# Two edge sums: fp32 rows stored in source order and gathered in destination order, in place of three bf16 parts scattered

## The chip, the cores and the metric

The kernel runs on one core of a Trainium2 chip. The metric is the time of one execution on the device, in microseconds.

## The reference, cut to what matters

A graph of 6250 nodes with 48 features and 200000 edges goes through four message-passing blocks, each followed by a layer norm. The change touches the last two, which are sums over edges of rows of x:

```python
def _L2_gnn_ref(x, edge_index, edge_weights):
    row, col = (edge_index[0], edge_index[1])
    ...
    norm = edge_weights / jnp.sqrt(deg[row] * deg[col])
    msg = x[row] * norm[:, None]
    out = jax.ops.segment_sum(msg, col, num_segments=N)

def _L3_gnn_ref(label_mat, edge_index, num_nodes):
    ...
    norm = deg_inv_sqrt[row] * deg_inv_sqrt[col]
    msgs = label_mat[row] * norm[:, None]
    out = jax.ops.segment_sum(msgs, col, num_segments=num_nodes)
```

The square roots of the degrees are multiplied into node rows before and after, so each block is: take the row y[src] of every edge (in the first of the two, times the edge's weight) and add it to the sum of dst.

## The kernel before, in words

The first phases (not touched, except for one) sort the edges into granules of GR = 4 edges that share a block of 128 nodes, once by source block and once by destination block. There are NS = 456 columns of 128 granules in either order. The phase edge_keys (called keys in the profile) computes these orders while GpSimd (POOL) gathers table rows, 34 columns a chunk, and ScalarE (ACT) stores them as raw. Its SyncE (SP) queue also fills tensors in DRAM with zeros, among them the whole of messages, k.msg: 171 stores of 384 KB at L334. k.place[p, u] is the place in destination order of a granule of the source order, k.origin the row in source order of a granule of the destination order.

The sums are the two stages at the end of program: next_tables (node rows y and their split in three bf16 parts, k.y3), then a spread, a tally, and combine. The weighted sum uses spread (stage 1), the plain sum spread_plain (stage 2); both are called spread in the profile.

Spread works in 76 chunks of EX = 6 columns, four chunks to a turn of the loop. For each chunk SP loads the one-hot matrices of the source lanes (oht, 384 KB); ACT reads a block number from irow and copies that block's three parts to table, six times; TensorE (PE) expands them to edges; VectorE (DVE) evicts; POOL scatters six times 128 granules to k.msg at place. In spread PE adds the three parts up in PSUM (72 matmuls of 48 columns a chunk, L2460), DVE multiplies by the weights (six at L2475) and splits the product again in three bf16 parts (split, L880 to L883) that go to out. In spread_plain PE passes the parts through (24 matmuls of 144 columns, L2566) and DVE copies them to out in 12 halves (L2582). POOL's scatters (L692) run after the copy of the chunk's part of place (L2478, L2578). out has a ring of four buffers, and DVE waits for the scatters of the chunk four before.

Tally also works in 76 chunks of six columns, two chunks to a turn. SP loads 864 KB of k.msg, in destination order and contiguous (L2615), DVE builds the one-hot matrices of the destination lanes (hot, 3072 elements a lane, L2650), PE sums with 72 matmuls of 48 columns (L2629), ACT evicts 288 elements to k.parts (L2639). POOL does nothing.

A phase of a different purpose, expand (L1506 to L1592, four times in the program), has nearly the structure that spread has after the change: 76 chunks of six columns, oht of 384 KB loaded by SP, 72 matmuls a chunk (of 52 columns), six evictions to fp32, and a 624 KB store by SP. Its table copies are shared between ACT and POOL, three each.

## Time and profile before

| | us |
|---|---|
| median of 3 runs | 19494.06 (19445.77 to 19525.49) |
| profiled execution, its own time | 19660.36 |
| span of the profiled execution | 19658.6 |
| spread 1 (weighted), first work to last landing | 17305 to 18053 |
| tally 1, up to its last eviction | 18053 to 18356 |
| spread 0 (plain) | 18450 to 19257 |
| tally 2 | 19257 to 19566 |

The span is the time between the first and the last instruction of one execution on the core; 1.8 us of its own time lie outside it. The stages run one after another with a barrier between, so what a stage gains or loses moves the end by as much. Busy time is summed by engine over a stretch; a group of instructions is one line, one operation and one shape.

### The profile page before, as it was taken

Reading aid. Unit: us, or ns where it says so; the run is one execution under the profiler, and the core shown is the slowest. Engines: PE = TensorE matmul, PEld = TensorE weight load, DVE = VectorE, ACT = ScalarE, POOL = GpSimd, SP = SyncE. Lnnn points to the kernel's source line nnn. Section 1 sums busy time; section 2 is a strip of 40 time slices with the busy share of each in tenths; the row PEclk is TensorE's granted clock in tenths of the full one; section 3 lists DMA queues with packets and bytes.
Section 4 is the critical chain, followed back from the end, with each engine's and each line's share of the span. In section 5 each row is a group of like instructions: output and inputs, shape, how many; then the busy total and the mean of one; then the engine's idle time right before and its main releaser. Section 6 shows DMA issues by size and latency. Waiting matters only on the chain. (4 is left out here: it accounts for less than half of the span.)

```text
span 19658.6 us, 403615 instructions
## 1 busy us (share of the span) xinstructions
PE 10605.2 (54%) x119643; PEld 8071.2 (41%) x119643; DVE 11207.2 (57%) x26701; ACT 5226.6 (27%) x15775; POOL 9060.3 (46%) x10645
## 2 busy tenths in 40 slices
PE   1001046666666337965884786598255555534334
PEld 1001024444444017864774776587233333323213
DVE  6557034445445456875886787588433333356647
ACT  0000012222222004642662454266122222211110
POOL 7778654444444623432441342244354545465251
PEclk9855555555555559987996997799666666655656
DMA  4552344444445227545552754655111111134434
GB/s 133 171 188 68 90 77 72 73 73 73 73 74 71 45 49 224 160 111 178 158 159 73 213 158 103 183 158 159 45 41 44 41 44 41 40 104 141 131 116 150
DMA packets 2548256, 2116.07 MB, mean 108 GB/s; under 512 B 418326, under 2 KB 2314030, under 8 KB 2541161
## 3 DMA queue, kind: packets, MB, share of 16 engines
q1 hardware_dynamic: 2164318, 1438.64, 25.0%
q0 software_dynamic: 309216, 539.49, 15.1%
q10 hardware_dynamic: 74552, 135.95, 2.1%
q8 instruction: 73, 1.20, 0.0%
q14 instruction: 97, 0.79, 0.0%
HBM read 1290.57 MB, written 726.03 MB: 103 GB/s over the span
## 5 line engine op out<-in xcount | busy, mean ns | idle before, releaser
L686 POOL DMA_INDIRECT attend_rows<-key_rows,attend_fetch_now x1824 | 1752.7, 961 | 2434.4 <-PE attend_seg L1717 2108.7
L686 POOL DMA_INDIRECT edges_rows<-raw,edges_perm_now x1824 | 1765.6, 968 | 2032.1 <-issue 1650.0
L1761 ACT ACTIVATE attend_hot<-attend_lane_hot,attend_share 128x128 f32<-128x128 fp8e4 x7296 | 2227.0, 387 | 110.6 <-DVE attend_share L1784 79.2
L686 POOL DMA_INDIRECT mlp_xin<-table,mlp_staged x1564 | 1492.1, 954 | 1483.7 <-PEq L2308 1023.5
L686 POOL DMA_INDIRECT keys_rows<-table,keys_staged x1564 | 1873.5, 1198 | 541.0 <-issue 541.0
L1717 PE MATMUL attend_seg<-attend_rows,attend_hot 128*128 128x49 f32 x14592 | 1884.3, 284 | 73.5 <-issue 39.1
L1717 PEld LDWEIGHTS attend_seg<-attend_rows,attend_hot 128*128 128x128 f32 x14592 | 1809.1, 201 | 115.2 <-issue 109.7
L1704 PE MATMUL attend_qx<-attend_table,attend_oht 128*128 128x90 bf16 x21888 | 1132.8, 211 | 441.7 <-DMA attend_oht<-src_hots 374.8
L692 POOL DMA_INDIRECT messages<-spread_out,spread_place_now x912 | 1024.8, 1124 | 603.0 <-issue 475.9
L1704 PEld LDWEIGHTS attend_qx<-attend_table,attend_oht 128*128 128x128 fp8e4 x21888 | 1036.7, 103 | 507.8 <-issue 506.4
L1801 DVE TENSOR_REDUCE attend_mraw<-attend_top 128x2 f32<-128x1024 f32 x912 | 1111.1, 1218 | 84.9 <-issue 48.4
L1093 PE MATMUL edges_ps_t<-ident,edges_attr 128*40 128x128 f32 x1824 | 430.4, 414 | 1232.8 <-issue 681.6
L2310 PE MATMUL mlp_ps<-mlp_xT,mlp_w 112*128 112x512 f32 (+1 forms) x828 | 598.9, 814 | 864.6 <-issue 776.5
L1211 DVE TENSOR_TENSOR edges_dot<-edges_ps_e,edges_rows 128x256 f32<-128x256 f32 x228 | 96.8, 425 | 1596.0 <-remote 1564.8
L1528 POOL COPY expand_table<-k 128x156 bf16 x912 | 291.3, 319 | 1527.1 <-PEq L1565 799.8
L1093 PEld LDWEIGHTS edges_ps_t<-ident,edges_attr 128*40 128x40 f32 x1824 | 244.3, 144 | 1681.3 <-issue 1607.1
L864 DVE TENSOR_TENSOR_SCAN mlp_sums<-keepr,mlp_sums,mlp_val 128x34 f32<-128x34 f32 x2208 | 502.4, 278 | 711.6 <-issue 707.9
L1577 PE MATMUL expand_ps<-expand_table,expand_oht 128*128 128x52 bf16 x21888 | 645.4, 188 | 474.4 <-DVE expand_out L1590 311.5
L1125 PE MATMUL edges_ps<-edges_eT,edges_w 40*48 40x512 f32 x912 | 831.2, 1056 | 47.7 <-issue 47.1
L1792 DVE TENSOR_REDUCE attend_score<-attend_prod 128x8 f32<-128x720 f32 x912 | 823.6, 903 | 31.5
L1590 DVE COPY expand_out<-expand_ps 128x208 f32<-128x208 f32 x1824 | 543.8, 366 | 502.4 <-DMA key_rows<-expand_out 300.1
L1110 PE MATMUL edges_ps<-edges_w,edges_act 49*128 49x48 f32 x3648 | 829.7, 412 | 0.0
(542 smaller groups left out, 23412.1 us busy)
## 6 DMA issues: line engine op xcount, KB each, us to landing
key_rows<-expand_out SPq DMA_DIRECT2D x304, 624.0 KB
attend_ea<-edge_attrs SPq DMA_DIRECT2D x912, 160.0 KB
tally_rows<-messages SPq DMA_DIRECT2D x152, 864.0 KB, 4.9
attend_table<-q SPq DMA_DIRECT2D x1832, 67.5 KB
expand_oht<-dst_hots SPq DMA_DIRECT2D x304, 384.0 KB
attend_oht<-src_hots SPq DMA_DIRECT2D x912, 128.0 KB
attend_lane_hot<-src_hots_by_edge SPq DMA_DIRECT2D x912, 128.0 KB
raw<-keys_rows ACTq DMA_DIRECT2D x46, 2176.0 KB
```

The source lines that it names most:

```text
L686: return nc.gpsimd.indirect_dma_start(out=out, out_offset=None, in_=table, in_offset=bass.IndirectOffsetOnAxis(ap=index, axis=0))
L692: return nc.gpsimd.indirect_dma_start(out=table, out_offset=bass.IndirectOffsetOnAxis(ap=index, axis=0), in_=rows, in_offset=None, bounds_ ...
L1093: ins = nc.tensor.transpose(ps_t[0:RBF, u, c * P:(c + 1) * P], attr[p][:, u, c * RBF:(c + 1) * RBF], k.ident[:])
L1110: ins = mm(ps_2[:, (u * GR + c) * F:(u * GR + c + 1) * F], act1[0:F + 1, u, c * P:(c + 1) * P], w2[:], start=True, stop=True)
L1125: ins = mm(ps_1[0:F, u, :], w1[:], eT[:, u, :], start=True, stop=True)
L1577: ins = nc.tensor.matmul(ps[u][:, c * KROW:(c + 1) * KROW], oht8[b][:, u, c::GR], table[b][:, u, j, :], start=(j == 0), stop=(j == 2))
L1704: ins = mm(qx[b % 2][:, u, c * QROW:(c + 1) * QROW], oht8[b][:, u, c::GR], table[b % 3][:, u, j, :], start=(j == 0), stop=(j == 2))
L1717: ins = mm(seg2[:, u, 0:SUMS], hot[p % 2][:, u, c, :], rows4[p][:, u, c, 0:SUMS], start=(c == 0), stop=(c == GR - 1))
L1761: ins = nc.scalar.activation(hot[p][:, u, c, :], lane_hot8[r][:, u, c, :], ACT.Copy, scale=share[p][:, u, c:c + 1])
L1792: ch.done(v.tensor_reduce(score[b % 3][:].rearrange("p u c -> p (u c)"), prod[:].rearrange("p u c w -> p (u c) w"), AX, ALU.add))
L1801: v.tensor_reduce(mraw[:], top[:], AX, ALU.max).then_inc(s_read, 1)
L2310: nc.tensor.matmul(ps_1[1 - q][:, 0:w], w1[:], xT[1 - q][0:X, 0:w], start=True, stop=True).then_inc(s_1, 1)
```

## The change

Both sums use one spread with fp32 output and one tally. Spread now evicts the 192 elements a lane and column to fp32 (times the weight in stage 1, a plain copy in stage 2), six instructions a chunk, and SP stores the chunk, 576 KB, in source order to k.rows_a, where each partition has its own contiguous stretch. POOL has no work there, and DVE no split. SP loads two chunks ahead and stores behind each load.

Tally's POOL gathers 128 granules of 768 bytes at a time from k.rows_a at k.origin, six times a chunk, into a ring of four fp32 buffers. ACT rounds the chunk (1152 elements a lane) to bf16, DVE subtracts that in place, ACT rounds the rest, DVE subtracts again into the third part. DVE's one-hot matrices are as before, between its two subtractions, and PE has the same 72 matmuls. DVE also copies the part of origin for the chunk three ahead, and ACT's eviction of the chunk before stands between its two roundings. Both loops have four chunks to a turn, with the first and last four outside the loop.

In edge_keys the 171 zero stores to k.msg are gone, and one store clears the row that each partition of k.rows_a has past its 456.

```diff
-MSG = 3 * F
-ZW = 1536
-ZEROS = NS * GR * MSG // ZW
-assert ZEROS * ZW == NS * GR * MSG and ZW // 2 <= C // 2 * F
...
-            with sp.Fori(0, ZEROS) as n:
-                sp.dma_start(k.msg.rearrange("(p u) w -> p (u w)", p=P)[:, bass.ds(n * ZW, ZW)], zeros[:, 0:ZW // 2].bitcast(BF16)).then_inc(s_out, 16)
+            sp.dma_start(k.rows_a.rearrange("(p r) w -> p r w", p=P)[:, NS, :], zeros[:, 0:GR * F]).then_inc(s_out, 16)
...
-def spread(nc, k):
+def spread(nc, k, weighted):
...
-        msg, rest = ph.sb("msg", [P, EX * GR, F]), ph.sb("rest", [P, EX * GR, F])
-        ring = range(RINGS)
-        out = [ph.sb(f"out{r}", [P, EX, GR * MSG], BF16) for r in ring]
-        place_now = ph.sb("place_now", [P, RINGS, EX], I32)
...
                 step(r, r, 0)
-            with eng.Fori(1, CHN // RINGS) as t:
+            with eng.Fori(1, CHN // RINGS - 1) as t:
                 for r in ring:
                     step(t * RINGS + r, r, t)
+            for r in ring:
+                step(CHN - RINGS + r, r, CHN // RINGS - 1)
 
         block = ph.block()
-
-        @block.gpsimd
-        def _(pool):
-            def step(n, r, t):
-                pool.wait_ge(s_now, n + 1)
-                pool.wait_ge(s_msg, n + 1)
-                pool.sem_inc(s_pool_turn, 1)
-                for u in range(EX):
-                    scatter(nc, k.msg, place_now[:, r, u:u + 1], out[r][:, u, :], NS * P - 1).then_inc(s_scat[r], 16)
-
-            steps(pool, step)
-            for r in ring:
-                pool.wait_ge(s_scat[r], 16 * EX * (CHN // RINGS))
 
         @block.sync
         def _(sp):
+            def load(n, b):
+                sp.dma_start(oht[b][:], k.oht_s.rearrange("(u p) w -> p u w", p=P)[:, bass.ds(n * EX, EX), :]).then_inc(s_load[b], 16)
+
+            def store(n, r):
+                sp.wait_ge(s_ev, (n + 1) * EX)
+                sp.dma_start(k.rows_a.rearrange("(p r) w -> p r w", p=P)[:, bass.ds(n * EX, EX), :], out[r][:]).then_inc(s_kept[r], 16)
+
             def step(n, r, t):
-                b = r % 2
-                after(sp, s_exp, (n - 1) * EX)
-                sp.dma_start(oht[b][:], k.oht_s.rearrange("(u p) w -> p u w", p=P)[:, bass.ds(n * EX, EX), :]).then_inc(s_load[b], 16)
-
+                if not isinstance(n, int) or n + 2 < CHN:
+                    sp.wait_ge(s_exp, (n + 1) * EX)
+                    load(n + 2, r % 2)
+                store(n, r)
+
+            for b in two:
+                load(b, b)
             steps(sp, step)
+            for r in ring:
+                sp.wait_ge(s_kept[r], 16 * (CHN // RINGS))
...
-            ch = Chain(dve, s_step)
-            by3 = [out[r][:].rearrange("p u (c j f) -> p (u c) j f", c=GR, j=3) for r in ring]
 
             def step(n, r, t):
+                after(dve, s_kept[r], t * 16)
                 for u in range(EX):
                     dve.wait_ge(s_exp, n * EX + u + 1)
-                    here, got = msg[:, u * GR:(u + 1) * GR, :], ps[u][:, 0:GR * F].rearrange("p (c f) -> p c f", f=F)
-                    v.tensor_tensor(here, got, bc(k.w_a[:, bass.ds((n * EX + u) * GR, GR)], F), ALU.mult).then_inc(s_ev, 1)
-                dve.wait_ge(s_ev, (n + 1) * EX)
-                after(dve, s_scat[r], t * (16 * EX))
-                v.tensor_copy(place_now[:, r], k.place[:, bass.ds(n * EX, EX)]).then_inc(s_now, 1)
-                split(v, ch, msg[:], [by3[r][:, :, j, :] for j in range(3)], rest[:])
-                dve.sem_inc(s_msg, 1)
-
-            for r in ring:
-                step(r, r, 0)
-            n0, per = ch.n, 4 * RINGS
-            with dve.Fori(1, CHN // RINGS) as t:
-                ch.n, ch.base = n0, (t - 1) * per
-                for r in ring:
-                    step(t * RINGS + r, r, t)
-                assert ch.n - n0 == per
-            dve.wait_ge(s_scat[0], 16 * EX * (CHN // RINGS))
-
-
-def spread_plain(nc, k):
+                    got = ps[u][:, 0:GR * F]
+                    if weighted:
+                        ins = v.tensor_tensor(out[r][:, u, :].rearrange("p (c f) -> p c f", f=F), got.rearrange("p (c f) -> p c f", f=F),
+                                              bc(k.w_a[:, bass.ds((n * EX + u) * GR, GR)], F), ALU.mult)
+                    else:
+                        ins = v.tensor_copy(out[r][:, u, :], got)
+                    ins.then_inc(s_ev, 1)
+
+            steps(dve, step)
+
+
+def tally(nc, k, tag):
...
+        rows = [ph.sb(f"rows{r}", [P, EX, GR * F]) for r in ring]
+        hot = [ph.sb(f"hot{b}", [P, EX * GR, P], BF16) for b in two]
+        parts3 = [ph.sb(f"parts3{b}", [P, 3, EX * GR * F], BF16) for b in two]
+        rest = [rows[r][:].rearrange("p u w -> p (u w)") for r in ring]
+        origin_now = ph.sb("origin_now", [P, RINGS, EX], I32)
...
                 pool.wait_ge(s_now, n + 1)
-                pool.wait_ge(s_msg, n + 1)
+                after(pool, s_low, n - RINGS + 1)
                 pool.sem_inc(s_pool_turn, 1)
                 for u in range(EX):
-                    scatter(nc, k.msg, place_now[:, r, u:u + 1], out[r][:, u, :], NS * P - 1).then_inc(s_scat[r], 16)
+                    gather(nc, rows[r][:, u, :], k.rows_a, origin_now[:, r, u:u + 1]).then_inc(s_rows[r], 16)
...
+                pe.wait_ge(s_low, n + 1)
...
-                            at = c * MSG + j * F
-                            ins = nc.tensor.matmul(ps[b][:, u * F:(u + 1) * F], hot[b][:, u * GR + c, :], rows[b][:, u, at:at + F],
+                            ins = nc.tensor.matmul(ps[b][:, u * F:(u + 1) * F], hot[b][:, u * GR + c, :], parts3[b][:, j, (u * GR + c) * F:(u * GR + c + 1) * F],
...
-            def step(n, b, t):
+            def evict(n, b):
                 act.wait_ge(s_seg, n + 1)
                 nc.scalar.activation(k.parts[:, bass.ds(n * (EX * F), EX * F)], ps[b][:, 0:EX * F], ACT.Copy).then_inc(s_ev, 1)
 
+            def step(n, r, t):
+                b = r % 2
+                act.wait_ge(s_rows[r], (t + 1) * (16 * EX))
+                after(act, s_seg, n - 1)
+                nc.scalar.activation(parts3[b][:, 0, :], rest[r], ACT.Copy).then_inc(s_high, 1)
+                if not isinstance(n, int) or n > 0:
+                    evict(n - 1, 1 - b)
+                act.wait_ge(s_rest, n + 1)
+                nc.scalar.activation(parts3[b][:, 1, :], rest[r], ACT.Copy).then_inc(s_mid, 1)
+
             steps(act, step)
+            evict(CHN - 1, 1)
             act.wait_ge(s_ev, CHN)
 
         @block.vector
         def _(dve):
             v = nc.vector
 
-            def step(n, b, t):
+            def listed(n, r):
+                v.tensor_copy(origin_now[:, r], k.origin[:, bass.ds(n * EX, EX)]).then_inc(s_now, 1)
+
+            def step(n, r, t):
+                b = r % 2
                 after(dve, s_seg, n - 1)
+                if not isinstance(n, int) or n + 3 < CHN:
+                    listed(n + 3, (r + 3) % RINGS)
+                dve.wait_ge(s_high, n + 1)
+                v.tensor_tensor(rest[r], rest[r], parts3[b][:, 0, :], ALU.subtract).then_inc(s_rest, 1)
                 v.tensor_tensor(hot[b][:], bc(k.dloc[:, bass.ds(n * (EX * GR), EX * GR)], P), rows_of(k.iota[:], EX * GR), ALU.is_equal).then_inc(s_hot, 1)
-
+                dve.wait_ge(s_mid, n + 1)
+                dve.wait_ge(s_hot, n + 1)
+                v.tensor_tensor(parts3[b][:, 2, :], rest[r], parts3[b][:, 1, :], ALU.subtract).then_inc(s_low, 1)
+
+            for r in range(3):
+                listed(r, r)
             steps(dve, step)
 
 
...
-    k.msg = dram("messages", [NS * P, GR * MSG], BF16)
+    k.rows_a = dram("rows_by_source", [P * (NS + 1), GR * F])
...
-                    (spread if stage == 1 else spread_plain)(nc, k)
+                    spread(nc, k, stage == 1)
```

How instructions move, at the places that matter. First VectorE in spread 1 before, one chunk (spread_ps is PSUM, w_a the weights, spread_out the scatter's source):

```order
L2475 TENSOR_TENSOR spread_msg<-spread_ps,w_a 128x192 x6
L2478 COPY spread_place_now<-place 128x6
L880 CAST spread_out<-spread_msg 128x24x48
L881 TENSOR_TENSOR spread_rest<-spread_msg,spread_out 128x1152
L882 CAST spread_out<-spread_rest 128x24x48
L883 TENSOR_TENSOR spread_out<-spread_rest,spread_out 128x24x48
```

Of these the first kind alone is left, now writing spread_out at once (L2467); the copy of place and the split are gone, and SyncE stores each chunk behind the load for two chunks later. GpSimd in the tally after the change, from its start:

```order
L2504 UNCONDITIONAL_BRANCH
L681 DMA tally_rows<-rows_by_source,tally_origin_now 128x192 x24
L2496 UNCONDITIONAL_BRANCH
L2496 ISA
L726 REGISTER_ALU
L681 DMA tally_rows<-rows_by_source,tally_origin_now 128x192 x6
L2507 REGISTER_ALU
```

GpSimd had nothing between spread and combine's part there; the 456 scatters stood in spread. The first four chunks stand ahead of the loop. VectorE in the tally's loop before, two chunks (hot0 and hot1 are the two buffers):

```order
L2605 ISA
L2650 ISA
L2650 TENSOR_TENSOR tally1_hot0<-dloc,iota 128x3072
L2650 ISA
L2650 TENSOR_TENSOR tally1_hot1<-dloc,iota 128x3072
L2605 REGISTER_ALU
```

and after the change, one chunk (tally_rows are the gathered fp32 rows, tally_parts the bf16 parts):

```order
L2555 ISA
L2555 COPY tally1_origin_now<-origin 128x6
L2562 REGISTER_ALU
L2563 TENSOR_TENSOR tally1_rows0<-tally1_rows0,tally1_parts30 128x1152
L2564 ISA
L2564 TENSOR_TENSOR tally1_hot0<-dloc,iota 128x3072
L2567 TENSOR_TENSOR tally1_parts30<-tally1_rows0,tally1_parts30 128x1152
```

Where one instruction a chunk stood, there are now four, on the engine and in the stage in which the gathers run.

## Rows read from the trace of the kernel before

**Rows 1.** the page, part 1: busy time of each engine, share of the span
```profile
PE 10605.2 (54%) x119643; PEld 8071.2 (41%) x119643; DVE 11207.2 (57%) x26701; ACT 5226.6 (27%) x15775; POOL 9060.3 (46%) x10645
```
**Rows 2.** stretches: length, busy PE, PEld, DVE, ACT, POOL, PEclk, DMA share, GB/s
```profile
17305.00:18053.00 748.00, 327.16 (x5472) 256.00 (x5472) 457.42 (x836) 147.16 (x456) 575.01 (x456) 0.51 0.35 119
18053.00:18356.00 303.00, 187.79 (x5472) 180.53 (x5472) 252.64 (x76) 31.26 (x76) 0.00 (x0) 0.77 0.71 222
18450.00:19257.00 807.00, 274.15 (x1824) 133.04 (x1824) 370.67 (x989) 147.12 (x456) 449.75 (x456) 0.51 0.32 110
19257.00:19566.00 309.00, 190.54 (x5472) 183.81 (x5472) 252.67 (x76) 31.26 (x76) 0.00 (x0) 0.75 0.70 218
12445.00:12701.00 256.00, 160.25 (x5472) 154.35 (x5472) 135.30 (x455) 74.62 (x224) 71.55 (x224) 0.96 0.99 301
17360.00:17400.00 40.00, 22.80 (x438) 19.27 (x436) 36.08 (x68) 10.98 (x34) 32.69 (x25) 0.50 0.37 125
```
**Rows 3.** groups in spread 1, 17305 to 18053; columns as in the page's part 5
```profile
L692 POOL DMA_INDIRECT messages<-spread_out,spread_place_now x456 | 575.0, 1261 | 217.1 <-issue 137.4 <-DVEq L2480 79.1 <-DVE spread_place_now L2478 0.6
L2460 PE MATMUL spread_ps<-spread_table,spread_oht 128*128 128x48 bf16 x5472 | 327.2, 212 | 500.5 <-issue 307.4 <-ACT spread_table L2444 118.4 <-DVE spread_msg L2475 73.2
...
L2444 ACT ACTIVATE spread_table<-y 128x144 bf16 x456 | 147.2, 323 | 570.1 <-PE spread_ps L2460 353.3 <-issue 185.3 <-remote 18.4
L2475 DVE TENSOR_TENSOR spread_msg<-spread_ps,w_a 128x192 f32<-128x192 f32 x456 | 129.0, 349 | 83.4 <-PE spread_ps L2460 40.8 <-remote 28.1 <-DVE spread_out L883 13.0
L883 DVE TENSOR_TENSOR spread_out<-spread_rest,spread_out 128x1152 bf16<-128x1152 f32 x76 | 103.3, 1359 | 2.6
```
**Rows 4.** timeline of PE in spread 1, one chunk's first and last matmuls
```profile
17366.32 1.92 PE L2460 MATMUL spread_ps<-spread_table,spread_oht 128*128 128x48 bf16 x44 [1.07 <-DVE spread_msg L2475]
...
17371.69 0.92 PE L2460 MATMUL spread_ps<-spread_table,spread_oht 128*128 128x48 bf16 x19 [0.49 <-issue]
```
**Rows 5.** timeline of ACT in spread 1: start, us, line
```profile
17373.64 0.32 ACT L2444 ACTIVATE spread_table<-y 128x144 bf16 x1 [3.13 <-PE spread_ps L2460]
17374.36 0.32 ACT L2444 ACTIVATE spread_table<-y 128x144 bf16 x1 [0.39 <-issue]
```
**Rows 6.** groups in spread 0, 18450 to 19257
```profile
L692 POOL DMA_INDIRECT messages<-spread_out,spread_place_now x456 | 449.8, 986 | 386.0 <-issue 338.5 <-DVE spread_place_now L2578 47.5
L2582 DVE CAST spread_out<-spread_ps 128x288 bf16<-128x288 f32 x912 | 355.6, 449 | 390.2 <-DMA attend_table<-q 295.7 <-PE spread_ps L2566 48.1 <-issue 42.7
```
**Rows 7.** groups in the first tally, 18053 to 18356
```profile
L2650 DVE TENSOR_TENSOR tally_hot<-dloc,iota 128x3072 bf16<-128x3072 f32 x74 | 246.0, 3356 | 42.3 <-PE tally_ps L2629 42.1 <-issue 0.2
L2629 PE MATMUL tally_ps<-tally_rows,tally_hot 128*128 128x48 bf16 x5472 | 187.8, 198 | 149.2 <-DMA tally_rows<-messages 141.5 <-ACT parts_sum L2639 7.4 <-issue 0.2
```
**Rows 8.** timeline of POOL and DVE at 1470 us: start, us, engine, line
```profile
1470.06 0.95 POOL L686 DMA_INDIRECT keys_rows<-table,keys_staged  x1 [0.30 <-issue]
...
1470.51 3.49 DVE L617 TENSOR_TENSOR keys_work<-keys_level,iota 114x3200 f32<-114x3200 f32 x1
1471.32 3.51 POOL L686 DMA_INDIRECT keys_rows<-table,keys_staged  x1 [0.31 <-issue]
...
1474.04 3.49 DVE L618 TENSOR_TENSOR keys_work<-keys_work,keys_jump 114x3200 f32<-114x3200 f32 x1
...
1475.13 3.23 POOL L686 DMA_INDIRECT keys_rows<-table,keys_staged  x1 [0.30 <-issue]
...
1478.66 0.94 POOL L686 DMA_INDIRECT keys_rows<-table,keys_staged  x1 [0.30 <-issue]
```
**Rows 9.** the gather's line L686: from issue to landing
```profile
DMA to landing us min/median/max: 2.3/2.5/2.6
```
**Rows 10.** groups of ACT in the keys phase, 0 to 2600
```profile
L363 ACT ACTIVATE keys_rows<-keys_attr 128x1360 f32<-128x1360 f32 x46 | 60.7, 1321 | 2.9 <-DMA keys_attr<-tail_attr 2.9
```
**Rows 11.** groups of the keys phase, 0 to 3600: the gathers
```profile
L686 POOL DMA_INDIRECT keys_rows<-table,keys_staged x1564 | 1873.5, 1198 | 541.0 <-issue 541.0
```
**Rows 12.** the keys phase: the zero stores' line L334
```profile
L334 SPq DMA_DIRECT2D messages<-keys_zeros x171: 3/700/1397, 521.0 to 1407.6; - x171
```

More of the change, by code:

```diff
@@ L2384, in _ @@
             v.tensor_copy(k.tail[:, 0:F], sums[1][:, C - 1, :]).then_inc(s_step, 1)
-def spread(nc, k):
+def spread(nc, k, weighted):
     CHN, RINGS = NS // EX, 4
     with ExitStack() as ctx:
-        ph = Phase(nc, ctx, "spread1")
-        two = range(2)
+        ph = Phase(nc, ctx, "spread1" if weighted else "spread0")
+        two, ring = range(2), range(RINGS)
         oht = [ph.sb(f"oht{b}", [P, EX, W // 2], BF16) for b in two]
@@ L2395, in spread @@
         table = [ph.sb(f"table{b}", [P, EX, 3, F], BF16) for b in two]
[L2396 to L2399 removed]
+        out = [ph.sb(f"out{r}", [P, EX, GR * F]) for r in ring]
         ps = [ph.ps(f"ps{u}", [P, 512]) for u in range(EX)]
[L2401 to L2402 removed]
+        s_table, s_exp, s_ev, s_pe_turn = (ph.sem(n) for n in ("s_table", "s_exp", "s_ev", "s_pe_turn"))
         s_load = [ph.sem(f"s_load{b}") for b in two]
[L2404 removed]
+        s_kept = [ph.sem(f"s_kept{r}") for r in ring]
         def steps(eng, step):
@@ L2514, in steps @@
                 step(r, r, 0)
-            with eng.Fori(1, CHN // RINGS) as t:
+            with eng.Fori(1, LOOPS - 1) as t:
                 for r in ring:
                     step(t * RINGS + r, r, t)
+            for r in ring:
+                step((LOOPS - 1) * RINGS + r, r, LOOPS - 1)
         block = ph.block()
@@ L2558, in step @@
                 b = r % 2
-                pe.wait_ge(s_load[b], (t * (RINGS // 2) + r // 2 + 1) * 16)
-                pe.wait_ge(s_table, n + 1)
-                for h in range(HALVES):
-                    q = (r * HALVES + h) % BANKS
-                    after(pe, s_ev, n * HALVES + h - BANKS + 1)
-                    pe.sem_inc(s_pe_turn, 1)
-                    for c in range(GR // 2):
-                        ins = nc.tensor.matmul(ps[q][:, c * MSG:(c + 1) * MSG], oht8[b][:, h // 2, (h % 2) * (GR // 2) + c::GR],
-                                               table[b][:, h // 2].rearrange("p j f -> p (j f)"), start=True, stop=True)
-                    ins.then_inc(s_exp, 1)
```

88 lines of the change are left out of this document (8 added, 80 removed).

## Prediction

> **What bounds the kernel now.** I began with the page's busy shares: no engine is over 57% [rows 1], so the share says nothing; the change is priced stage by stage. The table of stretches came next. The two spreads and tallies are 748, 303, 807 and 309 us, 2167 together, with a barrier between [rows 2]. The groups of each stage say which wait ends last. In spread 1 a scatter takes 1261 ns and VectorE is busy 457 of 748 us; VectorE waits for PE and the scatters' ring, so GpSimd and VectorE share the bound [rows 2, 3]. In spread 0 the same scatter takes 986 ns, and VectorE's evictions have the ring before them: its DMA side is the bound, 807 / 76 = 10.6 us a chunk [rows 2, 6]. In the tallies PE waits 141 us for rows, beside 76 one-hot instructions of 3.36 us on VectorE: a chunk is 4.0 us [rows 2, 7].
>
> **Spread.** Removed: 912 scatters, all splits (of which L883 alone is 103 us [rows 3]) and the ring's wait. Added: a 576 KB store a chunk on SyncE's queue, behind a load of 384 KB. What is left, per chunk:
> - transfers: 960 KB at the 301 GB/s of expand [rows 2] is 3.3 us. Expand moves 1008 KB a chunk in 256 / 76 = 3.4 us [rows 2], with SyncE issuing the same two transfers, so their queue is no bound.
> - VectorE: 6 x 0.349 = 2.1 us [rows 3]; the plain copies are smaller than the 449 ns of a 288-element one [rows 6].
> - ACT's table copies start 0.72 us apart [rows 5], 6 x 0.72 = 4.3, with the chunk's turn 4.4 us. (In expand GpSimd takes half of them; here it doesn't.)
> - PE: a chunk's 72 matmuls run from 17366.32 to 17372.61, 6.3 us, although the 44 first take 1.92 [rows 4]; over 40 us, 438 matmuls make 6.1 chunks, 6.6 us each [rows 2]. The idle time inside is "issue", 307 us in the stage [rows 3]: PE waited for nothing visible. This loop has four chunks to a turn; that of expand, two to a turn, shows none such and takes 3.4.
>
> The store, an edit of unseen cost here, is hidden by ACT's 4.4 on expand's evidence; without that cover it is 3.3. So a chunk is between 4.4 (ACT) and 6.6 (PE as seen). VectorE was 90% busy in those 40 us [rows 2], and part of PE's 6.6 was its waiting for that, which the change removes; the issue gaps aren't VectorE's. I take 5.6, between the two: 76 x 5.6 + 10 for start and end = 436 us a stage. Term: 872 - (748 + 807) = **-683**. Ends: 344 and 512 a stage.
>
> **Tally.** Removed: the 864 KB load. Added to each chunk: six gathers on GpSimd, two roundings on ACT, two subtractions on VectorE and a copy of six numbers. A gather alone is 0.95 us with 0.30 between two [rows 8]: 6 x 1.25 = 7.5 us, 3.5 over the present chunk. VectorE: 3.36 + 2 x 1.36 (L883, the same shape [rows 3, 7]) + 0.2 = 6.3. ACT: 1360 elements take 1.32 [rows 10], so 1152 about 1.12, twice, and the eviction 0.4: 2.7. PE: 188 / 76 = 2.5 at granted clock 0.77 [rows 2], at 0.5 some 3.8. GpSimd is the bound even undisturbed.
>
> It is disturbed. VectorE's instruction at 1470.51 reads two tensors in SBUF and ends at 1474.00; the gather that starts in it at 1471.32 takes 3.51 and ends 0.83 after it. The next pair does the same (3.23, ending 0.83 after 1477.53). The gather that began before it (1470.06) takes 0.95, and the one inside a reduction with one source (1478.66) 0.94 [rows 8]. The new subtractions and the one-hot instruction are all of the held kind. The 1261 against 986 ns of the scatters, beside subtractions in spread 1 and evictions from PSUM in spread 0, say the same [rows 3, 6]. The Trainium skill's page "SBUF — State Buffer", section "Who interferes with whom", infers that a tensor_tensor does not stall descriptor generation, which writes only; by that a chunk would be 7.5 and the time the first rival's 19359, and the rows of 1470 us speak against it.
>
> Walk one chunk from the end of the last gather: its rows are there at 2.0 (2.5 from issue [rows 9]), high rounding to 3.3, first subtraction to 4.65, one-hot to 8.0, second subtraction to 9.4; the middle rounding lies under the one-hot. The next gathers start at 0.3, 1.55, 2.8; the fourth at 4.05 falls in the first subtraction and ends 4.65 + 0.83 = 5.5; the fifth, at 5.8, falls in the one-hot and ends 8.8; the sixth, at 9.1, in the second subtraction and ends 10.2. That is the period: 10.2, the 7.5 and three holds of 2.7 together. With the landing moved by a few tenths the same walk gives 10.1 to 11.2. I take 10.4: 76 x 10.4 + 10 = 800 a stage. Term: 1600 - (303 + 309) = **+988**. Ends: 580 + 10 if nothing is held, 861 by the worst walk.
>
> The copy of origin (0.2 on VectorE, three chunks ahead), the queue's end waits and the stores' last landing cost nothing or are in the 10: VectorE has 4 us a chunk free. Without that cover the copy would be 2 x 76 x 0.2 = 30.
>
> **Keys.** The 171 zero stores lie between 521 and 1408 us [rows 12], but GpSimd's 1564 gathers take 1873.5 + 541.0 us and run on long after [rows 11]. At most the idle over 0.30 each comes back: 541 - 469 = 72. The gathers' time over 0.95 is VectorE's holding, which stays. I take **-20**, with -80 (the 72 and some) and +40 (gathers that fall differently into VectorE's instructions) as ends. The one store that clears the spare row is hidden by the same gathers; bare, it would be one transfer of a few us.
>
> **Sum.** -683 + 988 - 20 = **+285**. The profiled execution took 19660.36, 166 over the median; the change is put on the median: 19494 + 285 = 19779, told as **19780**. About 0.5% (97 us) is what a measurement of this kernel can tell from no change.
>
> **The rivals.**
> - *Gathers aren't held* (faster). The instructions of 1470 us write fp32 and the one-hot writes bf16, and half of each tally could find gathers already begun. Then a chunk is 7.5, a tally 590: 2 x 590 - 612 = 568, and -683 + 568 - 20 = -135, or 19359. It decides at a chunk of 8.5 us, where 2 x (76 x 8.5 + 10) - 612 meets the 703 gained; held time must stay under 1.0 us a chunk. For it: the reduction of the same length held nothing. Against it: both rows of two-source instructions, and the scatters' 1261. 14%.
> - *Spread at ACT's pace*: PE's issue gaps go with VectorE's split, and a chunk is 4.4. Then 344 a stage: -867 + 988 - 20 = +101, or 19595; with 10.0 in the tally, 19535. For it: expand shows 3.4. Against it: the gaps end on nothing that VectorE does. 19%. The Trainium skill's page on the runtime ("Runtime: NRT & Kernel Launch", section "Instruction fetch mechanics") gives PE room for 2048 instructions, refilled in blocks; by its number a body of four chunks, about 600 instructions, would fit, the gaps would not be fetching, and the time would be this rival's 19595; the gaps in the trace stand in such a body, and nothing in it says whether they are fetching.
> - *The gaps come to the tally*, whose PE loop now has four chunks to a turn in place of two. In spread 1 busy and issue are 327 + 307 = 634, 8.4 us a chunk [rows 3]. Then from the third part: PE 8.4, the eviction 0.4 that stands before the middle rounding on ACT, that rounding 1.1, the second subtraction 1.4: 11.4 us, 875 a tally, and 285 + 150 = +435, or 19930. 11%.
> - That the change doesn't do what it says: the same three bf16 parts are made from the same fp32, and the scatters are gone from the program; I give it nothing.
>
> **How the numbers follow.** The forecast case has 56%: 19780, its own range 19650 to 19900 (spread 5.0 to 6.6, tally 10.1 to 10.9). The range takes in the second and third rival and leaves out the first: 19440 to 20050. Faster by over 0.5%: the first rival, 0.14. Within 0.5% (19397 to 19591): about half the second rival and the low edge of the forecast, 0.14. Slower: the rest, 0.72.
>
> **What would show it.** In the changed profile: 456 gathers in each tally, mean near 1.4 us in place of 0.95, those begun inside a VectorE instruction ending 0.83 us after it; tallies of about 800; SyncE stores of 576 KB, spreads of about 436 with PE's idle put down to issue; if it is put down to ACT and the spreads are 344, the second rival holds. Gathers of 0.95 throughout and tallies under 650 would make the prediction wrong; so would PE's groups in the tally with issue idle of hundreds of us, the third rival's sign.

## The result and the profile after

The changed kernel took 19808.78 us (median of 4, 19803.13 to 19813.43) against 19509.78 for the kernel before in the same comparison (19445.77 to 19533.92): 299 us slower, ratio 1.0151 (95% interval 1.0136 to 1.0165). Forecast: +285, 19780.

The table of stretches of the changed kernel, its profiled execution (span 19805.5; columns as in [rows 2]: length, PE, PEld, DVE, ACT, POOL, PEclk, DMA share, GB/s), spread 1, tally 1, spread 0, tally 2:

```profile
17167.00:17579.00 412.00, 216.68 (x5472) 209.00 (x5472) 160.21 (x460) 147.18 (x456) 0.00 (x0) 0.60 0.53 182
17579.00:18394.00 815.00, 245.04 (x5472) 226.34 (x5472) 461.95 (x302) 199.73 (x228) 658.66 (x456) 0.55 0.25 55
18488.00:18899.00 411.00, 216.51 (x5472) 208.76 (x5472) 159.55 (x456) 147.20 (x456) 0.00 (x0) 0.60 0.53 182
18899.00:19715.00 816.00, 245.41 (x5472) 226.45 (x5472) 461.91 (x305) 199.61 (x228) 658.83 (x456) 0.55 0.24 55
```

Against [rows 2] the spreads gained 336 and 396 us (732, forecast 683), the tallies lost 512 and 507 (1019, forecast 988). The two spans differ by only 147 us, since the profiled execution of before spent 138 us more ahead of spread 1 (17305 against 17167) nearly all in stages that the change doesn't touch; this is most of the 166 by which it lay over the median. The stages' own sum, 1019 - 732 = 287, is nearer to the 299 of the medians.

Groups of spread 1 after the change, which answer to [rows 3]:

```profile
L2452 PE MATMUL spread_ps<-spread_table,spread_oht 128*128 128x48 bf16 x5472 | 216.7, 209 | 304.3 <-ACT spread_table L2436 296.2 <-issue 8.1
...
L2467 DVE TENSOR_TENSOR spread_out<-spread_ps,w_a 128x192 f32<-128x192 f32 x456 | 159.8, 358 | 248.5 <-PE spread_ps L2452 210.2 <-issue 0.2
L2436 ACT ACTIVATE spread_table<-y 128x144 bf16 x456 | 147.2, 323 | 269.2 <-issue 194.1 <-PE spread_ps L2452 62.1 <-PEq L654 13.1
```

PE's idle time put down to issue (it waited for nothing that the profile shows) fell from 307 us to 8. What is left is 296 us of waiting for ACT's table copies, yet ACT is busy 147 of 412 us. Its timeline:

```profile
17400.56 0.32 ACT L2436 ACTIVATE spread_table<-y 128x144 bf16 x1 [0.39 <-issue]
17402.51 0.32 ACT L2436 ACTIVATE spread_table<-y 128x144 bf16 x1 [1.63 <-PE spread_ps L2452]
17403.22 0.32 ACT L2436 ACTIVATE spread_table<-y 128x144 bf16 x1 [0.39 <-issue]
...
17407.73 0.32 ACT L2436 ACTIVATE spread_table<-y 128x144 bf16 x1 [1.31 <-PE spread_ps L2452]
```

Copies start 0.72 apart inside a chunk, as in [rows 5], but 1.95 and 1.64 us pass before the first of a chunk. The view gives PE as what ended that idle time; ACT's own register loads of the block number (source line L2435; count, then shortest/median/longest in ns) say otherwise. The load ahead of the copy at 17402.51 starts 0.1 us after the last copy of the chunk before has ended, so ACT wasn't waiting for PE then:

```profile
L2435 ACTq TENSOR_LOAD <-irow x1: 1111/1111/1111, 17401.0 to 17401.0; - x1
```

and the five after it:

```profile
L2435 ACTq TENSOR_LOAD <-irow x5: 274/277/284, 17402.6 to 17405.5; - x5
```

About one load a chunk takes 1.0 to 1.3 us in place of 0.28. In this spread 79 of the 456 loads took over 0.6 us, 44 of them the first of a chunk and 16 the second. Half of these long loads end 2.85 to 3.1 us after SyncE has issued a chunk's 384 KB load, which the 576 KB store follows 0.6 us later; the spread before, which had no such store, had 18 loads over 0.6 us and none over 0.75. So ACT is hardly ever free: 5 x 0.72 and one long step of 1.6 to 1.95 make 5.2 to 5.55 us, and the chunk takes 5.37 (403 us from the first copy to the last, over 75 chunks).

Groups of tally 1 after the change, which answer to [rows 7]:

```profile
L681 POOL DMA_INDIRECT tally_rows<-rows_by_source,tally_origin_now x456 | 658.7, 1444 | 599.1 <-DVE tally_origin_now L2555 460.4 <-issue 138.7
L2524 PE MATMUL tally_ps<-tally_parts,tally_hot 128*128 128x48 bf16 x5472 | 245.0, 215 | 571.4 <-DVE tally_parts L2567 558.8 <-issue 8.4
...
L2567 DVE TENSOR_TENSOR tally_parts<-tally_rows,tally_parts 128x1152 bf16<-128x1152 f32 x76 | 103.2, 1358 | 59.5 <-ACT tally_parts L2544 59.1
```

GpSimd's gathers take 1444 ns on the mean where a gather alone takes 950, and 0.30 lies between two. No gap between two gathers of either tally is longer, so GpSimd never waits: its 456 gathers fill 797 of the 815 us. One chunk's timeline, without SyncE (start, us, engine, line; gathers that aren't held are left out):

```profile
17805.19 1.36 DVE L2567 TENSOR_TENSOR tally_parts<-tally_rows,tally_parts 128x1152 bf16<-128x1152 f32 x1 [0.77 <-ACT tally_parts L2544]
...
17806.69 3.25 PE L2524 MATMUL tally_ps<-tally_parts,tally_hot 128*128 128x48 bf16 x72 [7.25 <-DVE tally_parts L2567]
...
17809.07 1.16 ACT L2540 ACTIVATE tally_parts<-tally_rows 128x1152 bf16<-128x1152 f32 x1 [3.91 <-DMA tally_rows<-rows_by_source,tally_origin_now]
17809.66 0.17 PEld L2524 LDWEIGHTS tally_ps<-tally_parts,tally_hot 128*128 128x128 bf16 x4 [0.21 <-issue]
...
17810.26 1.36 DVE L2563 TENSOR_TENSOR tally_rows<-tally_rows,tally_parts 128x1152 f32<-128x1152 f32 x1 [3.63 <-issue]
17811.43 1.01 POOL L681 DMA_INDIRECT tally_rows<-rows_by_source,tally_origin_now  x1 [0.30 <-issue]
17811.54 3.35 DVE L2564 TENSOR_TENSOR tally_hot<-dloc,iota 128x3072 bf16<-128x3072 f32 x1
17812.75 2.96 POOL L681 DMA_INDIRECT tally_rows<-rows_by_source,tally_origin_now  x1 [0.30 <-issue]
17814.23 0.41 ACT L2534 ACTIVATE parts_sum<-tally_ps 128x288 f32 x1 [4.00 <-DMA attend_lane_hot<-src_hots_by_edge]
17814.54 1.16 ACT L2544 ACTIVATE tally_parts<-tally_rows 128x1152 bf16<-128x1152 f32 x1
17815.73 1.36 DVE L2567 TENSOR_TENSOR tally_parts<-tally_rows,tally_parts 128x1152 bf16<-128x1152 f32 x1 [0.84 <-ACT tally_parts L2544]
17816.01 1.90 POOL L681 DMA_INDIRECT tally_rows<-rows_by_source,tally_origin_now  x1 [0.30 <-issue]
```

The gather at 17811.43 starts in the first subtraction, 0.19 us before its end, and ends 0.82 after it. The gather at 17812.75 starts inside the one-hot instruction (17811.54, to 17814.89), takes 2.96 and ends 0.82 after it; the one at 17816.01 starts inside the second subtraction (to 17817.09) and takes 1.90. All three are held as in [rows 8]. Over both tallies, all 385 gathers begun inside one of these three instructions and over 0.2 us before its end are held; of 63 begun in its last 0.2 us 20 are; of the 464 begun outside them none is.

But ACT's eviction at 17814.23 comes 4.5 us after the start of PE's last matmul (17809.75, in the row at 17806.69), and the middle rounding stands behind it. (The view puts ACT's idle time down to a DMA; what ACT waits for there is PE's semaphore.) The second subtraction therefore starts 0.84 us after the one-hot instruction has ended, and the chunk takes 10.55 us. The keys phase's gathers, which answer to [rows 11]:

```profile
L681 POOL DMA_INDIRECT keys_rows<-table,keys_staged x1564 | 1865.4, 1193 | 533.5 <-issue 533.5
```

The last of them starts at 2547.7, before the change at 2552.0; on the second chip below the two are 2547.8 and 2548.8.

### The profile page after: what moved, and what is told of

Its sections match the earlier page's. It is cut to its first block and busy times, and to the rows that moved or that the text cites. A ratio compares the mean times of both kernels' runs of the same rounds, so it can differ in the third digit from the quotient of the medians.

```text
span 19805.5 us, 405718 instructions
## 1 busy us (share of the span) xinstructions
PE 10580.4 (53%) x123291; PEld 8202.0 (41%) x123291; DVE 11120.5 (56%) x26245; ACT 5576.0 (28%) x16079; POOL 9350.5 (47%) x10645
## 5 line engine op out<-in xcount | busy, mean ns | idle before, releaser
L681 POOL DMA_INDIRECT tally_rows<-rows_by_source,tally_origin_now x912 | 1317.5, 1445 | 1187.0 <-DVE tally_origin_now L2555 909.6
L2524 PE MATMUL tally_ps<-tally_parts,tally_hot 128*128 128x48 bf16 x10944 | 490.5, 215 | 1143.7 <-DVE tally_parts L2567 1116.2
L2524 PEld LDWEIGHTS tally_ps<-tally_parts,tally_hot 128*128 128x128 bf16 x10944 | 452.8, 118 | 1181.4 <-DVE tally_parts L2567 884.7
```

The source lines that it names most:

```text
L681: return nc.gpsimd.indirect_dma_start(out=out, out_offset=None, in_=table, in_offset=bass.IndirectOffsetOnAxis(ap=index, axis=0))
L2524: ins = nc.tensor.matmul(ps[b][:, u * F:(u + 1) * F], hot[b][:, u * GR + c, :], parts3[b][:, j, (u * GR + c) * F:(u * GR + c + 1) * F], st ...
```

## The experiments

All runs are set against the kernel before on their own chip. It took 16798 us on the chip of the first four runs, 19522 on that of the next four and 19695 on that of the last four, so absolute times are compared only within a group of four. The durations of stages are compared across chips where the text says so.

**The changed kernel and the kernel before, unchanged, on a second chip.**

> The kernel before, profiled on the chip of these runs. The chip of the first four runs gave 16798 us for it where the first chip gave 19510, and the new tally's chunks were 9.85 us there in place of 10.5. Theory 'slow matmul completion': the difference lies in stretches where PE's results come late; the spreads before (748 and 807 us) would be shorter on a chip that does not show it, by the gaps put down to issue, and the new spreads (407) the same. If so the old spreads take 600 to 700 us here and the change costs more than 299 us. Rival: the difference lies only in stages that the change does not touch, and the four stages of before are 2167 us on any chip.

> The changed kernel on the same chip: spreads 405 to 410 us each, tallies 765 each if its chunks are 9.85 us (evictions at once), 806 to 815 if they are 10.5 (evictions 4.4 us late). Against before: 350 to 450 us slower on a chip of the second kind, 300 on one of the first.

Ratio 1.0155 (1.0135 to 1.0176), +301 us. The four stretches of before on that chip:

```profile
17176.00:17929.00 753.00, 323.75 (x5472) 254.32 (x5472) 458.53 (x836) 147.20 (x456) 566.95 (x456) 0.50 0.35 118
17929.00:18230.00 301.00, 191.55 (x5472) 184.18 (x5472) 252.94 (x76) 30.88 (x76) 0.00 (x0) 0.74 0.72 224
18327.00:19124.00 797.00, 275.65 (x1824) 132.36 (x1824) 369.38 (x988) 147.12 (x456) 448.69 (x456) 0.51 0.32 111
19124.00:19428.00 304.00, 188.52 (x5472) 181.68 (x5472) 252.42 (x76) 30.85 (x75) 0.00 (x0) 0.77 0.72 221
```

and of the changed kernel:

```profile
17177.00:17588.00 411.00, 215.26 (x5472) 207.70 (x5472) 159.38 (x456) 147.20 (x456) 0.00 (x0) 0.62 0.53 182
17588.00:18401.00 813.00, 246.18 (x5472) 226.42 (x5472) 461.13 (x304) 199.41 (x228) 658.33 (x456) 0.55 0.26 55
18498.00:18909.00 411.00, 214.15 (x5472) 206.58 (x5472) 158.75 (x456) 147.23 (x456) 0.00 (x0) 0.61 0.53 182
18909.00:19722.00 813.00, 246.23 (x5472) 226.65 (x5472) 461.09 (x304) 199.47 (x228) 658.32 (x456) 0.55 0.25 55
```

The first work of spread 1 starts at 17176 and 17177 here, so these two traces can be subtracted: -342, +512, -386, +509, together +293, and the spans differ by 294. The stages are the whole effect, and all four repeat those of the first chip within 10 us. The question in the first expectation, what the old spreads take where nothing comes late, stayed open, since evictions came late on this chip too.

**A probe for the late evictions.** SyncE has no work in the tally, so it can wait for PE's semaphore too:

```diff
+        @block.sync
+        def _(sp):
+            def step(n, r, t):
+                sp.wait_ge(s_seg, n + 1)
+                sp.sem_inc(s_seen, 1)
+            steps(sp, step)
```

> SyncE, idle in the tally, also waits for each chunk's matmuls and counts; nothing else changes. In the changed kernel ACT's eviction starts 4.4 us after the start of the chunk's last matmul, while before the change it started 0.3 after it. Theory A (the matmuls really end late, or their semaphore comes late): SyncE's wait is over at the same time as ACT's, some 4.4 us after the last matmul's start. Theory B (ACT itself is held up): SyncE's wait is over within 0.3 us. Either way the tallies stay at 806 and 815 us.

On this chip there was nothing late. PE's matmuls, ACT's high rounding and eviction:

```profile
15323.28 3.05 PE L2532 MATMUL tally_ps<-tally_parts,tally_hot 128*128 128x48 bf16 x72 [6.69 <-DVE tally_parts L2575]
...
15325.80 1.16 ACT L2548 ACTIVATE tally_parts<-tally_rows 128x1152 bf16<-128x1152 f32 x1 [6.11 <-DMA tally_rows<-rows_by_source,tally_origin_now]
...
15326.87 0.39 ACT L2542 ACTIVATE parts_sum<-tally_ps 128x288 f32 x1
```

and the moment at which SyncE's wait was over (first and last start of the line):

```profile
L2519 SPq EVENT_SEMAPHORE  x1: 17/17/17, 15326.4 to 15326.4; - x1
```

Over both tallies SyncE's wait is over at most 0.25 us after the start of a chunk's last matmul. A chunk takes 9.85 us and a tally 765, not the 806 and 815 expected. The time, 17232 us (one run), is 434 over the kernel before. The same kernel on a chip that gives 19.7 ms for the kernel before:

> The probe of the first experiment once more, since its chip did not show late evictions. If this chip gives 19.5 ms for the kernel before, evictions come 4.4 us after the last matmul's start again. Theory A (matmuls end late or their semaphore comes late): SyncE's wait for the same semaphore is over together with ACT's. Theory B (ACT is held up): SyncE's wait is over within 0.3 us. If the chip gives 16.8 ms, both come at once and the tallies are 765 again.

```profile
17855.56 0.31 PE L2532 MATMUL tally_ps<-tally_parts,tally_hot 128*128 128x48 bf16 x6 [0.27 <-issue]
...
17861.61 0.41 ACT L2542 ACTIVATE parts_sum<-tally_ps 128x288 f32 x1 [4.29 <-DMA attend_lane_hot<-src_hots_by_edge]
```

```profile
L2519 SPq EVENT_SEMAPHORE  x1: 17/17/17, 17861.5 to 17861.5; - x1
```

The last matmul starts at 17855.69 (in the first row), SyncE's wait is over at 17861.5 and ACT's eviction follows at 17861.61: both waiters are released together, 5.8 us late (the median of both tallies is 4.4). Theory A holds: the completion that PE signals is late, and ACT isn't the cause. This run took 19954 us (one run), its tallies 796 and 818 (first gather to last eviction).

Theory A has two readings, and the same trace bears on them. In 21 chunks of its first tally PE's own matmul records are spread over more than 5 us, mostly 6.4, in place of 3.2, and in 19 of these the eviction follows the last of them within 0.4 us: 6.8 us after the subtraction's end, where the chunks with compact records and a late eviction have 7.8. So the time goes by either in the records or behind them, which speaks for matmuls that are done late more than for a signal that is late. No run separates the two.

The last two chunks of the changed kernel, beside which no gather runs, have no such delay (eviction 3.16 us after the last subtraction, against 7.7), so on these chips the lateness goes with the gathers in this kernel.

**The middle rounding ahead of the eviction.**

```diff
-                if not isinstance(n, int) or n > 0:
-                    evict(n - 1, 1 - b)
                 act.wait_ge(s_rest, n + 1)
                 nc.scalar.activation(parts3[b][:, 1, :], rest[r], ACT.Copy).then_inc(s_mid, 1)
+                if not isinstance(n, int) or n > 0:
+                    evict(n - 1, 1 - b)
```

> ACT rounds the middle part first and evicts the chunk before after that. Theory 'held gathers' (GpSimd is the bound, and loses what VectorE's two-source instructions hold it): the second subtraction follows the one-hot instruction at once, by a walk of the gathers a chunk is 9.8 us in place of 10.5, each tally 55 shorter, the kernel 110 us faster (19700). Rival 'eviction chain' (matmuls, 4.4 us of wait, eviction, rounding, subtraction in a ring, 10.5 us): the ring is cut, so the tally would fall much further if that alone were the bound, towards 8 us a chunk, 400 us faster. No change at all would mean that the wait is only moved to the next chunk's first rounding.

17202 us, ratio 1.0229 (1.0201 to 1.0258); the probe's one run on the same chip took 17232. The tallies stay at 763, since no eviction was late here. On the third chip:

> The middle rounding ahead of the eviction, on a chip with late evictions: the second subtraction no longer waits for the eviction, a chunk is 9.85 us as on the other chip, each tally 50 shorter, the kernel 100 us faster than the changed one (19720). If late completions hold up something else too, less. On a chip of 16.8 ms: no change again.

19866 us, ratio 1.0084 (1.0062 to 1.0106) where the changed kernel had 1.0151 and 1.0155. The first tally:

```profile
17742.00:18506.00 764.00, 257.44 (x5472) 229.98 (x5472) 461.28 (x304) 207.85 (x228) 608.93 (x456) 0.55 0.27 59
```

764 in place of 813 to 815, and the second the same. Evictions are still late in it (7.85 us after the subtraction's end, against 6.2 on the chip above); nothing waits behind them now. Set against the probe's one run on this chip, the tallies, 762 by the same measure, are 34 and 56 us shorter and the time 88 (100 expected); set against the changed kernel on the other two chips, about 50 a tally. GpSimd goes from gather to gather with 0.30 between in both kernels. What the late eviction cost therefore shows as holding: 1335 ns a gather here, 1444 there, and 456 x 0.109 = 50 us.

**The one-hot's row of numbers in PSUM** (source numbers, a copy of iota; the instruction has one SBUF source left):

```diff
-                v.tensor_tensor(hot[b][:], bc(k.dloc[...], P), rows_of(k.iota[:], EX * GR), ALU.is_equal)
+                v.tensor_tensor(hot[b][:], rows_of(numbers[:, 0:P], EX * GR), bc(k.dloc[...], P), ALU.is_equal)
```

> The one-hot instruction reads its row of numbers from PSUM, so it has one source in SBUF in place of two. Held gathers: no gather begun inside it takes over 1.0 us, only the two subtractions hold; a chunk is 8.3 to 9.3 us, tallies 640 to 710, the kernel 200 to 330 us faster. Eviction chain: VectorE's sources don't matter, the ring of 10.5 us stays, and so do the tallies (806).

17044 us, ratio 1.0136 (1.0107 to 1.0165), 158 faster than the run with the middle rounding first, whose tallies equal the changed kernel's on this chip. A tally takes 685 (expected 640 to 710); the gain of the whole is under the 200 to 330 expected, which counted from tallies of 806. One chunk:

```profile
15250.37 3.35 DVE L2565 TENSOR_TENSOR tally_hot<-tally_numbers,dloc 128x3072 bf16<-128x3072 f32 x1
...
15251.57 0.94 POOL L681 DMA_INDIRECT tally_rows<-rows_by_source,tally_origin_now  x1 [0.30 <-issue]
15252.82 0.94 POOL L681 DMA_INDIRECT tally_rows<-rows_by_source,tally_origin_now  x1 [0.30 <-issue]
15253.83 1.36 DVE L2568 TENSOR_TENSOR tally_parts<-tally_rows,tally_parts 128x1152 bf16<-128x1152 f32 x1
15254.07 1.94 POOL L681 DMA_INDIRECT tally_rows<-rows_by_source,tally_origin_now  x1 [0.30 <-issue]
```

The one-hot takes 3.35 us as before, and two gathers begin inside it and take 0.94; the one begun inside the subtraction at 15253.83 still takes 1.94. In each tally all 148 gathers begun inside the one-hot instruction take under 1.0 us, where in the changed kernel all 75 were held. So the holding goes with the place of one operand. GpSimd still never waits: 456 x (1.147 + 0.30) = 660 of the 685 us. The rival of this expectation was not there to be refuted: on this chip no eviction is late.

**One-hot matrices made for two chunks alone** (74 of 76 left out):

```diff
+                if isinstance(n, int) and n < 2:
                     v.tensor_tensor(hot[b][:], ...)
+                else:
+                    dve.sem_inc(s_hot, 1)
```

> The one-hot matrices are made for the first two chunks of a tally alone; those of the other 74 are left out. Held gathers: as with the row of numbers in PSUM or a little better, 8 to 9 us a chunk. Eviction chain: 10.5 us stay, with VectorE almost idle.

16866 us (one run), a tally 617, 8.0 us a chunk. GpSimd's row of it:

```profile
L681 POOL DMA_INDIRECT tally_rows<-rows_by_source,tally_origin_now x456 | 453.2, 994 | 597.5 <-DVE tally_origin_now L2555 458.8 <-issue 138.6
```

994 ns, almost a gather alone (the subtractions still hold some): 6 x (0.99 + 0.30) = 7.75 us, what GpSimd asks for, and the chunk is near it. Here too evictions are punctual, so the run speaks for the gathers' side alone.

**GpSimd copies half of the tables in spread** (its loop is ACT's, for u from 0 to 2; PE waits for both).

```diff
+        @block.gpsimd
+                after(pool, s_exp, (n - 1) * EX)
+                for u in range(EX // 2):
+                    block_i = pool.value_load(...)
+                    ins = nc.gpsimd.tensor_copy(table[b][:, u], ...)
+                ins.then_inc(s_taken, 1)
-                for u in range(EX):
+                for u in range(EX // 2, EX):
```

> GpSimd, idle in the new spread, copies three of the six table blocks of each chunk, as in expand. ACT is the bound (six copies 0.72 us apart and one register load of 1.1 us in place of 0.28 make 5.35 us a chunk, PE waits for ACT 296 of 521 us): a chunk falls to 3.3 to 3.7 us, each spread to 260 to 290, the kernel 240 to 290 us faster than the changed one. Theory of the prediction (PE's gaps of issue are the bound, 5.6 us a chunk): PE's gaps stay and each spread remains near 400.

19542 us, ratio 1.0008 (0.9995 to 1.0021): 281 faster than the changed kernel beside it and equal to the kernel before. Spread 1:

```profile
17174.00:17438.00 264.00, 154.87 (x5472) 148.75 (x5472) 143.22 (x456) 73.64 (x228) 70.03 (x228) 0.96 0.84 282
```

264 us, 3.5 a chunk, in place of 411. ACT was the bound, not PE's supply of matmuls. PE now waits most for the 384 KB loads (154 us of the stage); its granted clock in the stretch is 0.96 in place of 0.62, with its work closer together.

**The zero stores put back.**

```diff
+            with sp.Fori(0, ZEROS) as n:
+                sp.dma_start(k.msg...[:, bass.ds(n * ZW, ZW)], zeros...).then_inc(s_out, 16)
```

> The 171 zero stores of 384 KB are put back into the keys phase (into a tensor that nothing reads), the rest is the changed kernel. The keys phase's last gather ended at 2551 before and 2547 after the change on the first chip: the stores are hidden under the gathers. Expected 0 to 20 us slower than the changed kernel; with -20 as the prediction had it, 20. If the stores delay other queues, up to 80.

19824 us against 19823, ratio 1.0149 (1.0125 to 1.0172); the last gather of keys starts at 2551.0 in place of 2547.8. They cost about 3 us in the keys phase, too little to be seen in the times.

**Three edits together: middle rounding first, numbers in PSUM, tables shared.**

> Three edits together: middle rounding first, the one-hot's row of numbers in PSUM, GpSimd with half of the table copies. Two gathers a chunk can still be held, by the subtractions alone: 8.0 to 8.8 us a chunk, tallies 620 to 680 in place of 813 (or 685 with the row in PSUM alone), spreads 262. On a chip of 19.5 ms: 19150 to 19270; the kernel before is beaten by 1.3 to 1.9%.

19502 us against 19695, ratio 0.9895 (0.9877 to 0.9914): faster than the kernel before by 1.05%, where 1.3 to 1.9 were expected. A tally takes 720, not 620 to 680. The expectation was too low from the start: the run with the numbers in PSUM took 685, with nothing late, and GpSimd's gathers alone filled 660 of it, which moving the rounding doesn't change. The rest is new. The gathers' mean is 1180 here (15 us a tally more), and GpSimd waits 25 and 29 us in the two tallies, which it did in none of those above, for buffers behind slow chunks of PE. VectorE's subtractions come 7.8 us apart in the median, but 11 intervals in one tally and 13 in the other are 12 to 26. In one of 24 us PE's matmuls come so:

```profile
18019.33 0.22 PE L2538 MATMUL tally_ps<-tally_parts,tally_hot 128*128 128x48 bf16 x1 [0.43 <-issue]
...
18020.02 0.28 PE L2538 MATMUL tally_ps<-tally_parts,tally_hot 128*128 128x48 bf16 x3 [0.47 <-issue]
...
18020.75 0.22 PE L2538 MATMUL tally_ps<-tally_parts,tally_hot 128*128 128x48 bf16 x1 [0.45 <-issue]
...
```

One to three matmuls every 0.72 us, beside undisturbed gathers of 0.95. The old spread's gaps look the same: between 17368.6 and 17371.7, in the chunk of [rows 4], its matmuls come in bunches 0.73 to 0.80 us apart. Where such a stretch outlasts the four buffers, GpSimd has to wait for it.

**fp32 matmuls on the gathered rows** (no roundings, no subtractions, one-hot matrices in fp32; numbers in PSUM, tables shared).

```diff
-                            ins = nc.tensor.matmul(ps..., hot[b][:, u * GR + c, :], parts3[b][:, j, ...], ...)
+                        ins = nc.tensor.matmul(ps..., hot[b][:, u * GR + c, :], rows[r][:, u, c * F:(c + 1) * F], ...)
```

> The tally without the split in three parts: 24 fp32 matmuls a chunk on the gathered rows, no roundings and no subtractions; the one-hot's row of numbers in PSUM, the table copies shared. No instruction of VectorE in the tally has two sources in SBUF, so no gather is held: 6 x (0.95 + 0.30) = 7.5 us a chunk, 575 to 590 a tally, unless the fp32 matmuls (0.28 us each before, in another stage) bound it at 24 x 0.28 = 6.8 us or more. 466 us faster than with the shared table copies alone: 19075 on a chip of 19.5 ms, 2.3% under the kernel before. If fp32 matmuls take over 0.32 us each, PE is the bound.

19668 us, ratio 0.9982 (0.9967 to 0.9997), a tally 800. PE's row in tally 1:

```profile
L2535 PE MATMUL tally_ps<-tally_rows,tally_hot 128*128 128x48 f32 x3648 | 778.9, 413 | 24.6 <-DMA tally_rows<-rows_by_source,tally_origin_now 14.6 <-issue 9.9
```

PE is busy 779 of 800 us. The profile has two records for each fp32 matmul, so these are 76 x 24 = 1824 matmuls of 0.43 us, at granted clock 0.50. PE is the bound, as the last clause of the expectation said, and the 466 us did not come: its 0.28 was the mean of one record, in a stage at granted clock 0.94. The gathers' mean is 0.95, none is held, and GpSimd waits 194 us.

## Why the prediction was right, point by point

- **Spread, -683 forecast, -732 measured** (5.37 us a chunk where I took 5.6). The size was near, the reason wrong. The step "the issue gaps aren't VectorE's" let PE's gaps stay; they went with the scatters and the split (307 us to 8), and the bound is ACT. The second rival named ACT, at 4.4 us: what it lacked is the register load that takes 1.1 us about once a chunk. The trace of before had it, in the stage that I took for evidence: in expand (12445 to 12701) 71 of ACT's 223 register loads take over 0.6 us. Sharing the copies gave 264 a stage, which shows the bound.
- **Tally, +988 forecast, +1019 measured** (10.55 us a chunk where I took 10.4). The mechanism is as forecast: gathers are held by VectorE's instructions with two sources in SBUF, to 0.82 us after their end, and GpSimd is the bound. On the chip without late completions the walked chunk of 10.2 measured 9.85. The step that failed is "the middle rounding lies under the one-hot": on the chip of the result it waits behind the late eviction. That closes a ring of 10.55 us (PE's completion 7.7 after the subtraction, eviction and its turn 0.3, rounding 1.2, subtraction 1.4), the third rival's with 7.7 in place of 8.4. GpSimd doesn't wait for the ring; the two go in step, and the later second subtraction lengthens the holding. With the ring cut the chunk is 9.85 again. The cause, late completion, isn't one that I had.
- **Keys, -20 forecast**, -4 and -1 measured in the two pairs of traces and 3 by the experiment: a term of the sum that was mis-sized, within its ends.
- **The first rival** (gathers not held) is refuted twice: by the rows of the timeline, and by the PSUM operand that frees the gathers. Its own sum had a slip: 76 x 7.5 + 10 is 580 and not 590, which puts it at 19339. The upper end of the forecast case was set too low for its chunks as well: 6.6 and 10.9 together give about 20010, not 19900.
- The Trainium skill's inference in "SBUF — State Buffer", "Who interferes with whom", that a tensor_tensor doesn't stall descriptor generation, disagrees with these gathers. The same section's statement that a VectorE instruction with at most one SBUF input, outside the 2-port modes, doesn't contend with GpSimd agrees with the one-hot instruction that has one operand in PSUM (148 gathers begun in it in each tally, none held).
- So the errors were 49 us one way and 31 and 16 the other, and they met: the stages and the keys sum to +283 for +285. That is luck. The 299 of the medians is 16 more, less than the 88 by which the runs of the kernel before differ.

Open: why PE's matmuls and completions come late beside gathers where the kernel before takes 19.5 to 19.7 ms, and not on the chip where it takes 16.8. The two traces of the probe's kernel, the same program on either kind of chip, show that it isn't a matter of these sums alone. In the earlier stage mlp, beside which GpSimd gathers too, PE's idle time put down to issue is nothing on the chip of 16.8 ms (first row) and 835 us on the other:

```profile
L2305 PE MATMUL mlp_ps<-mlp_xT,mlp_w 112*128 112x512 f32 (+1 forms) x828 | 467.3, 649 | 0.0
L2305 PE MATMUL mlp_ps<-mlp_xT,mlp_w 112*128 112x512 f32 (+1 forms) x828 | 596.0, 811 | 920.2 <-issue 835.3 <-ACT mlp_xT L2333 84.8
```

The new spreads, which have no gathers, take 405 to 408 us on both. On the chip of 16.8 ms the probe's kernel was 434 us over the kernel before, more than 299, though its tallies were shorter. By the sum of its four stages (406 + 409 + 764 + 765 = 2344) the old ones took about 1910 there, against 2155 to 2167; that is an estimate, since the kernel before wasn't profiled on that chip. If it is right, the old spreads' issue gaps are of the same kind. Why a register load takes 1.1 us wasn't tried either.

## What to carry to other kernels

Before moving indirect DMAs next to VectorE work, list that stage's instructions with two SBUF sources: each held a GpSimd gather begun inside it until its own end and 0.82 us more, and an operand that can live in PSUM freed it (765 to 685 us a tally). Then add the gathers up: where GpSimd never waits, their count times their mean and the 0.30 between is the stage (660 of 685 us), and edits that leave the holding alone gain nothing. When an engine moves out of a stage, give it the work of whichever engine is next: three table copies a chunk on the idle GpSimd paid back 281 of the 301 us. And keep an eviction out of the queue position ahead of an instruction that the next step waits for (34 to 56 us a tally, where completions come late).

## What the runs showed of the hardware that I had not expected

- PE's completion was seen 4.4 to 5.8 us after the start record of its last matmul while gathers ran, where the kernel before takes 19.5 to 19.7 ms; within 0.25 us on the chip of 16.8, and in the last chunks of a tally, without gathers. PE's records alone mostly don't show it; a second engine waiting for the same semaphore does.
- On those chips PE at times gets one to three matmuls every 0.72 us, for up to 23 us.
- A register load by ACT that takes 0.28 us took 1.0 to 1.3 about once a chunk in the new spread, mostly ending 2.4 to 3.1 us after SyncE issued the chunk's 384 KB load.
- The kernel before took 16.8 ms on one chip and 19.5 to 19.7 on the others. The change cost 1.5% on the latter; on the former the two variants with tallies as long as the changed kernel's there cost 2.3 and 2.6%.
